# Loading the attention stacks in two halves, the first one slot earlier

## The chip, the cores and the metric

The kernel runs on one core of a Trainium2 chip. The time is the device time of one execution in microseconds; given is the median of three runs. Engines: TensorE (PE, matmuls; PEld is its weight load), VectorE (DVE), ScalarE (ACT), GpSimd (POOL) and SyncE (SP), which here issues all DMA transfers.

## The reference

The input x has 16 batches of 256 tokens with 128 channels. Eight residual blocks follow each other, each on a layer norm of x: a wide attention (16 heads of 64), experts, an attention with heads of eight and a slope bias, experts, a rotary attention with heads of eight, a group attention, a gated recurrence, and the group attention again. The change touches the four attentions with heads of eight. Cut to what matters:

```python
# slope: 16 heads of 8, causal, bias = m * (key - query)
score = einsum('bqhd,bkhd->bhqk', q, k) / sqrt(128) + bias          # causal
# rope: q and k rotated by position, 4 key heads for 16 query heads, causal, output projection
scores = einsum('bqhd,bkhd->bhqk', q, k) * 8 ** -0.5                # causal
# group (twice): a token sees the keys of its own group only; the first 5 tokens see both
l = where(key_mask, einsum('bqhd,bkhd->bhqk', q * scale, k), -inf)
a = softmax(l); out = einsum('bhqk,bkhd->bqhd', a, v)
```

Each of the four is followed by softmax and the product with v.

## The kernel before

The whole program is one launch with a block of instructions per layer, for each engine a list in program order; semaphores order the engines among each other. The four attentions come from one function, `narrow_attention`, with `kind` "slope", "rope" or "group".

**The stack.** A head of eight would fill 8 of TensorE's 128 rows. So q and k in float32 are split into three bf16 parts ("high", "mid", "low"), and for each pair of heads (there are `PAIRS` = 8 pairs, `z` = 0, 1 within a pair, in partitions 0 to 63 and 64 to 127) six combinations of parts are laid below each other: 48 rows that give the product to nearly float32 precision. Below them stand rows for the causal mask, the slope, the group masks (`sp_masks`) and three rows for the row maxima ("shift"). This tile is `st`, with `KEEP` = 3 buffers, index `b % KEEP`; per batch it has two sides (q and k), eight pairs and 256 tokens.

**How it is filled.** POOL writes the parts (`parts`, lines 1014 to 1019). SyncE writes them to a DRAM tensor, `stack_dram`, in rearranged order (pieces "high", "mid", "low", line 613), waits until all six transfers have landed (`parted`) and loads the 48 rows of the stack from there (piece "stack", line 618): one transfer for each `z`, 384 KB each, 4 KB contiguous for each row and side. It also waits until the scores of the batch that used the buffer before are done:

```python
wait(sp, s["scored"], PAIRS * (b - KEEP + 1))
```

In the group layers four transfers of mask rows (line 597) follow behind the stack. The "shift" piece (line 626) writes the row maxima to DRAM, "spread" (line 631) loads them into `st`.

**How it is used.** TensorE computes for each pair i of batch b the "max" piece (line 699: q times k, whose row maxima VectorE takes, line 906) and two batches later the "score" piece (line 720: k times q, with the maxima in the shift rows, which ScalarE puts through exp, line 834), then "value" (line 740). Max 0 of a batch waits for the stack (`landed`) and, in the group layers, for the masks (`masked`); score 0 waits for the spread.

**The order.** `NARROW_ORDER` gives for each kind and engine eight slots; slot i of round n holds score i of batch n and beside it pieces of other batches, as ("piece", index, offset of the batch). The two lines below, of the slope layer, say that SyncE loads the stack of batch n+2 in slot 0 and that TensorE does max 0 of batch n+2 in slot 4 (slot 3 in the rope layer, 4 in the group layers), max 4 in slot 7:

```python
            [("stack", 0, 2)],
            [("score", 4, 0), ("max", 0, 2), ("turnmax", 0, 1), ("turn1", 0, -2), ("max", 1, 2), ("v", 0, 2)],
```

The first `HOSTED` = 2 batches of a layer are prepared while the layer before it runs (`FIRST`).

Of the kernel before, what the change touches and what calls it, by code (L numbers as in the profile page):

```python
# [54 lines left out]
def wait(eng, sem, value):  # L55

    if isinstance(value, int) and value <= 0:
        return
    eng.wait_ge(sem, value)
# [144 lines left out]
def norm_stats(K, s, split=False):  # L204
# [26 lines left out]
    def on_scalar(act):  # L231
# [9 lines left out]
KEEP = 3  # L241
AHEAD = 4
QUADS = H // 4
PAIRS = H // 2
# [50 lines left out]
            [],  # L295
        ],
        "sp": [
            [("stack", 0, 2)],
            [],
            [],  # L300
            [],
            [("shift", 0, 1), ("high", 0, 3)],
            [("mid", 0, 3)],
            [("spread", 0, 1), ("low", 0, 3)],
            [],
        ],
    },
    "rope": {
# [38 lines left out]
            [],  # L347
        ],
        "sp": [
            [("stack", 0, 2)],  # L350
            [],
            [],
            [],
            [("shift", 0, 1), ("high", 0, 3)],
            [("spread", 0, 1)],
            [("mid", 0, 3), ("low", 0, 3)],
            [],
        ],
    },
    "group": {  # L360
# [38 lines left out]
            [("reg_v", 0, 2)],  # L399
        ],  # L400
        "sp": [
            [("stack", 0, 2)],
            [],
            [],
            [],
            [],
            [("shift", 0, 1), ("high", 0, 3)],
            [("spread", 0, 1)],
            [("mid", 0, 3), ("low", 0, 3)],
        ],  # L410
    },
}
# [13 lines left out]
HOSTED = 2  # L426
# [12 lines left out]
FIRST["group"] = FIRST["slope"]  # L439
for _kind in FIRST:  # L440
    FIRST[_kind]["pool"] = [("parts", 0, 0), ("parts", 0, 1)]
    FIRST[_kind]["sp"] = [(_what, 0, _b) for _b in range(HOSTED) for _what in ("high", "mid", "low", "stack")]


EXPERT_HOST = {
# [19 lines left out]
def narrow_attention(nc, K, kind, name, W):  # L465
# [9 lines left out]
    ROW_EXTRA = PARTS * D8  # L475
# [11 lines left out]
    with ExitStack() as ctx:  # L487
        ctx.enter_context(nc.cleanup_on_exit())

        def sb(n, shape, dt=F32):  # L490
# [3 lines left out]
            "stat_dve", "var_ready", "rstd_ready", "norm_ready", "first_dve", "first_var", "first_rstd", "first_norm",  # L494
            "weights", "set_pe", "set_act", "set_pool", "kept0", "kept1", "rows",
            "xn", "full0", "full1", "drained0", "drained1",
            "rotated", "summed", "part", "parted0", "parted1", "landed0", "landed1", "masked0", "masked1", "masked2", "pool_own", "dve_own",
            "maxima", "maxed", "joined", "split", "shifted0", "shifted1", "spread0", "spread1",
            "scored", "exps", "valued", "taken", "biased", "added", "stats",
            "reg_q", "reg_v", "reg_max", "reg_sum", "reg_new", "reg_probs", "reg_out")}  # L500
        full, drained = [s["full0"], s["full1"]], [s["drained0"], s["drained1"]]
        parted, landed = [s["parted0"], s["parted1"]], [s["landed0"], s["landed1"]]
        shifted, spread = [s["shifted0"], s["shifted1"]], [s["spread0"], s["spread1"]]
        masked = [s["masked0"], s["masked1"], s["masked2"]]

# [6 lines left out]
        st = sb("st", [P, KEEP, 2, PAIRS, S], BF16)  # L512
# [51 lines left out]
        LANDED = 16 * 2  # L564
# [35 lines left out]
        def sp_piece(sp, what, i, b):  # L600
            par, turn = b % 2, b // 2
            if what in ("high", "mid", "low"):
                part = ("high", "mid", "low").index(what)
                to = K.stack_dram[par].rearrange("a n d z j s -> a (d z j) n s")
                q_at = (slice(0, 3), slice(3, 6, 2), slice(4, 5))[part]
                k_at = (slice(2, 5), slice(1, 6, 4), slice(0, 1))[part]
                repeat = (3, 2, 1)[part]
                sp.wait_ge(s["part"], 3 * b + part + 1)
                if part == 0:
                    wait(sp, landed[par], LANDED * turn)  # L610
                for which, slots in ((0, q_at), (1, k_at)):
                    src = parts[:, par, part, which, :].unsqueeze(1).to_broadcast([P, repeat, S])
                    sp.dma_start(to[which, :, slots, :], src).then_inc(parted[par], 16)  # L613
            elif what == "stack":
                sp.wait_ge(parted[par], 96 * (turn + 1))
                wait(sp, s["scored"], PAIRS * (b - KEEP + 1))
                for z in range(2):
                    sp.dma_start(st[64 * z:64 * z + ROW_EXTRA, b % KEEP].rearrange("p a j s -> p a (j s)"),
                                 K.stack_dram[par][:, :, :, z].rearrange("a n d j s -> (n d) a (j s)")).then_inc(landed[par], 16)
                if kind == "group" and b >= HOSTED:  # L620
                    sp_masks(sp, b)
            elif what == "shift":
                m, filling = fill["turnmax", b]
                sp.wait_ge(drained[m], filling)
                wait(sp, spread[par], 32 * turn)
                sp.dma_start(K.shift_dram[par].rearrange("r z j s -> (r z j) s"), rows[:, par, :]).then_inc(shifted[par], 16)
            elif what == "spread":
                sp.wait_ge(shifted[par], 16 * (turn + 1))
                for z in range(2):
                    at = slice(64 * z + ROW_SHIFT, 64 * z + ROW_SHIFT + 3)  # L630
                    sp.dma_start(st[at, b % KEEP, 0].rearrange("p j s -> p (j s)"),
                                 K.shift_dram[par][:, z].rearrange("r j s -> r (j s)")).then_inc(spread[par], 16)
# [25 lines left out]
        def pe_piece(pe, what, i, b):  # L658
# [23 lines left out]
            elif what == "max":  # L682
                if i == 0:
                    if b == 0:
                        pe.wait_ge(s["rows"], ROWS_LANDED)
                        pe.wait_ge(s["weights"], 1)
                        wait(pe, s["set_act"], {"slope": 1, "group": 1, "rope": 2}[kind])
                    pe.wait_ge(landed[b % 2], LANDED * (b // 2 + 1))
                    if kind == "group":
                        pe.wait_ge(masked[b % KEEP], 64 * (b // KEEP + 1))  # L690

                wait(pe, s["maxed"], PAIRS * b + i - (1 if b == 0 else 0))
                Mx = max_bank(i, b)
                for t in range(NT):
# [49 lines left out]
            elif what in ("turn0", "turn1"):  # L744
                k = 0 if what == "turn0" else 1
                pe.wait_ge(s["taken"], 2 * b + k + 1)
                for t in range(NT):
                    for g in range(2):
                        ins = pe.transpose(bank[:, (2 * t + g) * P:(2 * t + g + 1) * P],  # L749
                                           ot[:, k, g * S + t * P:g * S + (t + 1) * P], K.ident[:])  # L750
                ins.then_inc(full[m], 1)
            elif what == "turnmax":
                pe.wait_ge(s["split"], b + 1)
                for t in range(NT):
                    ins = pe.transpose(bank[0:48].bitcast(BF16)[:, t * P:(t + 1) * P],
                                       cols[:, b % 2, t].rearrange("p r z j -> p (r z j)"), K.ident16[:])
                ins.then_inc(full[m], 1)
            elif what == "attn":
                for k in ("turn0", "turn1"):
                    pe.wait_ge(drained[fill[k, b][0]], fill[k, b][1])  # L760
                for t in range(NT):
                    ins = pe.transpose(bank[:, t * P:(t + 1) * P], att[:, b % 2, t, :], K.ident[:])
                ins.then_inc(full[m], 1)
            elif what == "project":
                pe.wait_ge(drained[fill["attn", b][0]], fill["attn", b][1])
                for t in range(NT):
                    ins = pe.matmul(bank[:, t * C:(t + 1) * C], att_t[:, b % 2, t * P:(t + 1) * P], W["out"], start=True, stop=True)  # L767
                ins.then_inc(full[m], 1)
            elif what == "reg_scores":
                pe.wait_ge(s["reg_q"], b + 1)  # L770
                pe.wait_ge(landed[b % 2], LANDED * (b // 2 + 1))
                pe.wait_ge(masked[b % KEEP], 64 * (b // KEEP + 1))
                pe.matmul(bank[0:RH, 0:S], qblk[:, b % 2, :], qk[:, b % 2, 1, :], start=True, stop=False)
                pe.matmul(bank[0:RH, 0:S], K.not_first[0:ROW_SHIFT, :], st[0:ROW_SHIFT, b % KEEP, 1, 0, :], start=False,
                          stop=True).then_inc(full[m], 1)
            elif what == "reg_turn":
                pe.wait_ge(s["reg_probs"], b + 1)
                for t in range(NT):
                    ins = pe.transpose(bank[:, t * RH:(t + 1) * RH], pxn[:, t * P:(t + 1) * P], K.ident[0:RH, 0:RH])
                ins.then_inc(full[m], 1)  # L780
            elif what == "reg_value":
                pe.wait_ge(drained[fill["reg_turn", b][0]], fill["reg_turn", b][1])
                pe.wait_ge(s["reg_v"], b + 1)
                for t in range(NT):
                    ins = pe.matmul(bank[:, 0:RH], vplain[:, t, :], pxt[:, t * RH:(t + 1) * RH],
                                    start=(t == 0), stop=(t == NT - 1))
                ins.then_inc(full[m], 1)
# [363 lines left out]
def groups(nc, K, name, W, following):  # L1151
# [3 lines left out]
    with ExitStack() as ctx:  # L1155
# [16 lines left out]
        sim, low, top = sb("sim", [P, TILES]), sb("low", [P, TILES]), sb("top", [P, TILES])  # L1172
# [7 lines left out]
        @block.sync  # L1180
        def _(sp):
            following.sp_first(sp)
            following.first("sp", sp, 8)

        def queries(n):
            return banks[2 + n % 2][:, 0:NT * (C + H)].rearrange("p (t c) -> p t c", t=NT)
# [328 lines left out]
def experts(nc, K, name, W, following):  # L1515
# [3 lines left out]
    with ExitStack() as outer:  # L1519
# [52 lines left out]
        @block.sync  # L1572
        def _(sp):
            following.sp_first(sp)
            following.first("sp", sp, 4 * HOSTED)

        @block.tensor
        def _(pe):
# [756 lines left out]
```

## Time and profile before

| what | value |
|---|---|
| median of three runs | 2356.72 us (2353.28 to 2361.72) |
| span of the profiled execution | 2348.3 us |
| TensorE busy, matmuls | 2052.1 us, 87% |
| TensorE weight loads | 1381.5 us, 59% |
| VectorE, ScalarE, GpSimd busy | 1544.7, 1199.0, 825.0 us |
| granted TensorE clock, mean | 0.932 |
| stack loads | 128 transfers of 384 KB, median 5.5 us to landing |

The profiled execution has no time of its own beside its span; the three runs are timed apart from it. Times in the rows are microseconds from the start of the span. In the span the slope attention runs from about 890 to 1135, the rope attention from 1375 to 1630, the two group attentions from 1680 to 1945 and from 2065 to 2335.

### The profile page before, as it was taken

What the parts mean: (1) busy time and instruction counts of PE and PEld (TensorE: products, weight loads), DVE (VectorE), ACT (ScalarE), POOL (GpSimd) and SP (SyncE); (2) the same over time, 40 slices, a digit from 0 to 9 for tenths busy, and PEclk for the clock granted to TensorE, in tenths of its full rate; (3) what the DMA queues carried; (4) which work ended last, traced back from release to release, by engine and by line L of the source; (5) the groups of instructions that cost most, each with busy time, mean ns of one, the idle gap of its engine ahead of it and who ended that gap; (6) DMA issues with size and microseconds to landing.
All of it is one profiled execution on the core that took longest, in us unless ns stands there. A gap on an engine that the chain in (4) does not pass through costs nothing. (4 is left out here: it accounts for less than half of the span.)

```text
span 2348.3 us, 52692 instructions
## 1 busy us (share of the span) xinstructions
PE 2052.1 (87%) x20735; PEld 1381.5 (59%) x20735; DVE 1544.7 (66%) x2742; ACT 1199.0 (51%) x2044; POOL 825.0 (35%) x1272
## 2 busy tenths in 40 slices
PE   6999999999959997998689989997599985479996
PEld 3666666666648995555578966664345543335553
DVE  5777777777743435666354447774688875768884
ACT  3444444444343324665623326655477776447774
POOL 4444444444423432332144414441233322433330
PEclk9999999999969998999789989998699997769998
DMA  5000000000000022444000214441244420134441
GB/s 167 1 1 1 1 1 1 1 1 1 1 6 2 14 46 70 113 113 99 2 4 1 55 29 113 113 112 32 70 100 115 113 61 1 42 80 107 113 109 46
DMA packets 142787, 120.97 MB, mean 52 GB/s; under 512 B 11808, under 2 KB 127408, under 8 KB 142548
## 3 DMA queue, kind: packets, MB, share of 16 engines
q1 hardware_dynamic: 142548, 117.64, 21.1%
q8 instruction: 167, 2.74, 0.5%
q14 instruction: 72, 0.59, 0.1%
HBM read 63.48 MB, written 54.12 MB: 50 GB/s over the span
## 5 line engine op out<-in xcount | busy, mean ns | idle before, releaser
L906 DVE TENSOR_REDUCE l_group_mx<-maxima 128x4 f32<-128x1024 f32 x248 | 304.0, 1226 | 69.0 <-PE maxima L699 67.5
L834 ACT ACTIVATE l_group_pr<-scores 128x1024 f32<-128x1024 f32 x256 | 261.5, 1021 | 71.7 <-PE scores L720 69.1
L2171 POOL TENSOR_TENSOR l_wide_tiles_sum<-l_wide_pr 128x256 f32<-128x256 f32 x256 | 180.7, 727 | 212.4 <-ACT l_wide_pr L2114 212.4
L2142 DVE RECIPROCAL l_wide_rc<-bank 128x256 f32<-128x256 f32 x128 | 223.8, 1749 | 8.4 <-PE bank L2075 7.9
L2114 ACT ACTIVATE l_wide_pr<-scores 128x512 f32<-128x512 f32 x256 | 139.1, 595 | 163.1 <-PE scores L2058 163.1
L2126 DVE TENSOR_REDUCE l_wide_mx<-maxima 128x2 f32<-128x512 f32 x248 | 159.4, 685 | 52.6 <-PE maxima L2038 52.0
L906 DVE TENSOR_REDUCE l_slope_mx<-maxima 128x6 f32<-128x768 f32 x124 | 118.9, 959 | 74.2 <-PE maxima L706 72.7
L2104 ACT ACTIVATE l_wide_qk<-bank 128x512 f32<-128x512 f32 x128 | 76.4, 597 | 175.2 <-PE bank L2025 175.2
L906 DVE TENSOR_REDUCE l_rope_mx<-maxima 128x6 f32<-128x768 f32 x124 | 118.8, 958 | 56.3 <-PE maxima L706 55.4
L834 ACT ACTIVATE l_slope_pr<-scores 128x768 f32<-128x768 f32 x128 | 103.5, 809 | 87.0 <-PE scores L727 86.8
L834 ACT ACTIVATE l_rope_pr<-scores 128x768 f32<-128x768 f32 x128 | 103.7, 811 | 77.0 <-PE scores L727 76.8
L740 PE MATMUL bank<-l_group_pr,va 128*32 128x256 f32 x2048 | 142.1, 397 | 0.0
L2069 PE MATMUL bank<-l_wide_pr,l_wide_va 128*64 128x256 f32 x1024 | 138.8, 392 | 0.0
L699 PE MATMUL maxima<-l_group_st 50*128 50x256 bf16 x992 | 101.8, 285 | 39.1 <-DVE l_group_mx L906 14.4
L2058 PE MATMUL scores<-l_wide_qk 64*128 64x256 f32 x1024 | 131.4, 376 | 0.0
L2166 POOL CAST l_wide_qk<-l_wide_qk 128x512 bf16<-128x512 f32 x128 | 78.1, 610 | 146.2 <-ACT l_wide_qk L2104 146.2
L1001 POOL CAST l_group_cols<-l_group_mx 128x32 bf16<-128x32 f32 x32 | 6.7, 209 | 318.8 <-DVE l_group_mx L906 318.8
L720 PE MATMUL scores<-l_group_st 53*128 53x256 bf16 x1024 | 102.6, 279 | 16.3 <-ACT l_group_pr L834 11.5
L2058 PEld LDWEIGHTS scores<-l_wide_qk 64*128 64x128 f32 x1024 | 98.6, 189 | 9.8
L1660 ACT ACTIVATE l_rope_e_ht<-maxima 128x512 f32<-128x512 f32 x64 | 38.2, 597 | 106.4 <-PE maxima L1612 106.0
L2025 PE MATMUL bank<-l_wide_xnt,w_q 128*128 128x256 f32 x256 | 90.3, 435 | 2.5 <-ACT l_wide_qk L2104 1.4
L1660 ACT ACTIVATE l_slope_e_ht<-maxima 128x512 f32<-128x512 f32 x64 | 38.2, 597 | 104.4 <-PE maxima L1612 104.1
(468 smaller groups left out, 4853.5 us busy)
## 6 DMA issues: line engine op xcount, KB each, us to landing
l_group_st<-stack_dram SPq DMA_DIRECT2D x64, 384.0 KB, 5.5
l_slope_st<-stack_dram SPq DMA_DIRECT2D x32, 384.0 KB, 5.6
l_rope_st<-stack_dram SPq DMA_DIRECT2D x32, 384.0 KB, 5.5
stack_dram<-l_group_parts SPq DMA_DIRECT2D x64, 192.0 KB, 2.3
stack_dram<-l_group_parts SPq DMA_DIRECT2D x64, 128.0 KB, 1.9
stack_dram<-l_slope_parts SPq DMA_DIRECT2D x32, 192.0 KB, 2.4
stack_dram<-l_rope_parts SPq DMA_DIRECT2D x32, 192.0 KB, 2.3
stack_dram<-l_slope_parts SPq DMA_DIRECT2D x32, 128.0 KB, 2.3
```

What stands on the lines that cost most here:

```text
L699: ins = pe.matmul(Mx[:, z, first:first + keys], st[at, b % KEEP, 0, i, t * P:(t + 1) * P], st[at, b % KEEP, 1, i, 0:keys], start=(t == 0 o ...
L720: ins = pe.matmul(Tp[:, z, t * S:t * S + S - first], st[at, b % KEEP, 1, i, t * P:(t + 1) * P], st[at, b % KEEP, 0, i, first:S], start=(t ...
L740: ins = pe.matmul(Ob[i // 2][32 * z:32 * z + 32, (i % 2) * S + first:(i % 2) * S + S], va[:, b % KEEP, t, h // G, :], pr[:, (h // 2) % AHE ...
L834: act.activation(pr[:, i % AHEAD, :, 0:keys], Tp[:, :, 0:keys], ACT.Exp).then_inc(s["exps"], 1)
L906: dve.tensor_reduce(mx[:, b % 2, :, :, i], max_bank(i, b)[:, :, 0:BLOCKS * keys].rearrange("p z (a k) -> p z a k", k=keys), AX.X, ALU.max, ...
L2025: ins = pe.matmul(bank[:, z * S:(z + 1) * S], w[:, i * P:(i + 1) * P], xnt[:, at, :], start=True, stop=True)
L2058: ins = pe.matmul(Tb[z][:, t * S:(t + 1) * S], qk[rows(z), at, i, 1, t * P:(t + 1) * P], qk[rows(z), at, i, 0, :], start=False, stop=(t == ...
L2069: ins = pe.matmul(Ob[i % 2][rows(z), 0:S], va[:, at, kt, 2 * i + z, :], pr[:, i % 2, z, kt * S:(kt + 1) * S], start=(kt == 0), stop=(kt == ...
L2114: act.activation(pr[:, i % 2, z, :], Tb[z][:], ACT.Exp).then_inc(s["exps"], 1)
L2126: dve.tensor_reduce(mx[:, at, :, 2 * i + z], max_banks(i, b)[z][:].rearrange("p (t k) -> p t k", k=S), AX.X, ALU.max, negate=True).then_in ...
L2142: own.done(dve.reciprocal(rc[:], Ob[i % 2][:, S:2 * S]))
L2171: pool.tensor_tensor(tiles_sum[:, i % 2, z, :], pr[:, i % 2, z, 0:S], pr[:, i % 2, z, S:2 * S], ALU.add).then_inc(s["added"], 1)
```

## The change

Each stack is loaded in two pieces. Piece 0 has pairs 0 to 3, piece 1 pairs 4 to 7; each is two transfers (one for each `z`) of 192 KB, with 2 KB contiguous for each row and side. Piece 1 stays in slot 0 of its round; piece 0 goes one slot ahead, to the end of slot 7 of the round before, where it only needs scores 0 to 3 of the batch that used the buffer. Each piece has a semaphore of its own. TensorE waits for piece 0 at max 0 and for piece 1 at max 4. The masks follow behind piece 1. The register scores of the group layers (`reg_scores`), which read pair 0, wait for piece 0.

```diff
         "sp": [
-            [("stack", 0, 2)],
+            [("stack", 1, 2)],
...
-            [],
+            [("stack", 0, 3)],
...
-            [("mid", 0, 3), ("low", 0, 3)],
+            [("mid", 0, 3), ("low", 0, 3), ("stack", 0, 3)],
...
-    FIRST[_kind]["sp"] = [(_what, 0, _b) for _b in range(HOSTED) for _what in ("high", "mid", "low", "stack")]
+    FIRST[_kind]["sp"] = [(_what, _i, _b) for _b in range(HOSTED) for _what, _i in (
+        ("high", 0), ("mid", 0), ("low", 0), ("stack", 0), ("stack", 1))]
...
                 if part == 0:
-                    wait(sp, landed[par], LANDED * turn)
+                    for half in range(2):
+                        wait(sp, landed[par][half], LANDED * turn)
...
             elif what == "stack":
+                half = slice(i * PAIRS // 2, (i + 1) * PAIRS // 2)
                 sp.wait_ge(parted[par], 96 * (turn + 1))
-                wait(sp, s["scored"], PAIRS * (b - KEEP + 1))
+                wait(sp, s["scored"], PAIRS * (b - KEEP) + half.stop)
                 for z in range(2):
-                    sp.dma_start(st[64 * z:64 * z + ROW_EXTRA, b % KEEP].rearrange("p a j s -> p a (j s)"),
-                                 K.stack_dram[par][:, :, :, z].rearrange("a n d j s -> (n d) a (j s)")).then_inc(landed[par], 16)
-                if kind == "group" and b >= HOSTED:
+                    sp.dma_start(st[64 * z:64 * z + ROW_EXTRA, b % KEEP, :, half].rearrange("p a j s -> p a (j s)"),
+                                 K.stack_dram[par][:, :, :, z, half].rearrange("a n d j s -> (n d) a (j s)")
+                                 ).then_inc(landed[par][i], 16)
+                if kind == "group" and b >= HOSTED and i == 1:
                     sp_masks(sp, b)
...
-                    pe.wait_ge(landed[b % 2], LANDED * (b // 2 + 1))
                     if kind == "group":
                         pe.wait_ge(masked[b % KEEP], 64 * (b // KEEP + 1))
-
+                if i % (PAIRS // 2) == 0:
+                    pe.wait_ge(landed[b % 2][i // (PAIRS // 2)], LANDED * (b // 2 + 1))
```

SyncE in a steady round of the rope layer, before. The waits are named after the first use of a semaphore, so `l1_slope_scored` is the count of scores done and the names that begin with `l0_wide` stand for the parts' semaphores. The stack waits for scores and parts, and then two transfers go out:

```order
L613 DMA stack_dram<-l_rope_parts 128x256 [waits l0_wide_summed]
L613 DMA stack_dram<-l_rope_parts 128x256
L618 DMA l_rope_st<-stack_dram 48x2x2048 [waits l1_slope_scored,l0_wide_biased]
L618 DMA l_rope_st<-stack_dram 48x2x2048
L626 DMA shift_dram<-l_rope_rows 48x256 [waits l1_slope_spread0,l0_wide_scored]
```

The same place with the change:

```order
L616 DMA stack_dram<-l_rope_parts 128x256 [waits l0_wide_summed]
L616 DMA stack_dram<-l_rope_parts 128x256
L622 DMA l_rope_st<-stack_dram 48x2x1024 [waits l1_slope_scored,l0_wide_divided]
L622 DMA l_rope_st<-stack_dram 48x2x1024
L622 DMA l_rope_st<-stack_dram 48x2x1024 [waits l1_slope_scored,l0_wide_divided]
L622 DMA l_rope_st<-stack_dram 48x2x1024
L631 DMA shift_dram<-l_rope_rows 48x256 [waits l1_slope_spread1,l0_wide_scored]
```

Between the same neighbours, the last part and the next shift, two transfers have become four of half the size, and each pair has its own wait for scores.

TensorE at the end of slot 7 of the rope layer, scores 7 and max 4, before:

```order
L720 MATMUL scores<-l_rope_st 128x256 [waits l1_slope_exps]
L720 MATMUL scores<-l_rope_st 128x256
L720 MATMUL scores<-l_rope_st 128x128 x2
L727 MATMUL scores<-corner_kq,choose 128x2x64 x4
L699 MATMUL maxima<-l_rope_st 128x128 [waits l1_slope_maxed]
```

And with the change:

```order
L725 MATMUL scores<-l_rope_st 128x256 [waits l1_slope_exps]
L725 MATMUL scores<-l_rope_st 128x256
L725 MATMUL scores<-l_rope_st 128x128 x2
L732 MATMUL scores<-corner_kq,choose 128x2x64 x4
L704 MATMUL maxima<-l_rope_st 128x128 [waits l1_slope_maxed,l1_slope_landed11]
```

TensorE's matmuls keep their order; max 4 has gained the wait for the second piece.

## Rows read from the trace of the kernel before

**Rows 1.** The page: span, and busy time, share and instructions of each engine
```profile
span 2348.3 us, 52692 instructions
...
PE 2052.1 (87%) x20735; PEld 1381.5 (59%) x20735; DVE 1544.7 (66%) x2742; ACT 1199.0 (51%) x2044; POOL 825.0 (35%) x1272
```

**Rows 2.** Waits of TensorE, whole span: us in total, times, longest us
```profile
PE maxima L699 <- DMA l_group_st<-mask_dram: 12.9, 4, 6.5
...
PE maxima L699 <- DMA l_rope_st<-stack_dram: 10.2, 12, 1.5
...
PE maxima L699 <- DMA l_slope_st<-stack_dram: 9.3, 11, 1.4
...
PE maxima L699 <- DMA l_group_st<-stack_dram: 7.6, 6, 1.9
...
PE maxima L699 <- issue: 3.1, 6, 0.7
```

**Rows 3.** Timeline, SyncE, slope and rope: start, us, line, op, out<-in, count
```profile
1013.53 0.80 SPq L618 DMA_DIRECT2D l_slope_st<-stack_dram  x2
1021.90 0.31 SPq L626 DMA_DIRECT2D shift_dram<-l_slope_rows  x1
...
1027.13 0.81 SPq L618 DMA_DIRECT2D l_slope_st<-stack_dram  x2
...
1084.81 0.81 SPq L618 DMA_DIRECT2D l_slope_st<-stack_dram  x2
...
1560.91 0.81 SPq L618 DMA_DIRECT2D l_rope_st<-stack_dram  x2
```

**Rows 4.** DMA issues, first and second transfer of 1013.53: KB, us to landing
```profile
l_slope_st<-stack_dram SPq DMA_DIRECT2D x1, 384.0 KB, 4.7
...
l_slope_st<-stack_dram SPq DMA_DIRECT2D x1, 384.0 KB, 6.3
```

**Rows 5.** Timeline, TensorE, slope: max 0, max 4, max 0, max 0 [idle before <-releaser]
```profile
1020.23 0.34 PE L699 MATMUL maxima<-l_slope_st 56*128 56x128 bf16 x4 [0.96 <-DMA l_slope_st<-stack_dram]
...
1026.27 0.34 PE L699 MATMUL maxima<-l_slope_st 56*128 56x128 bf16 x4
...
1076.93 0.34 PE L699 MATMUL maxima<-l_slope_st 56*128 56x128 bf16 x4
...
1091.56 0.34 PE L699 MATMUL maxima<-l_slope_st 56*128 56x128 bf16 x4 [0.98 <-DMA l_slope_st<-stack_dram]
```

**Rows 6.** Timeline, TensorE, rope: max 0 of two rounds in a row
```profile
1553.02 0.33 PE L699 MATMUL maxima<-l_rope_st 50*128 50x128 bf16 x4
...
1568.43 0.34 PE L699 MATMUL maxima<-l_rope_st 50*128 50x128 bf16 x4 [1.23 <-DMA l_rope_st<-stack_dram]
```

**Rows 7.** Timeline, SyncE, a group round: the stack and the masks
```profile
1843.51 0.81 SPq L618 DMA_DIRECT2D l_group_st<-stack_dram  x2
1844.36 1.21 SPq L597 DMA_DIRECT2D l_group_st<-mask_dram  x4
```

**Rows 8.** Windows, same round: us, busy (x) by engine, PEclk, DMA share, GB/s
```profile
1850.00:1850.50 0.50, 0.50 (x7) 0.14 (x5) 0.23 (x2) 0.46 (x1) 0.32 (x2) 1.00 0.12 28
```

**Rows 9.** Timeline, TensorE, same round: max 0
```profile
1851.24 0.39 PE L699 MATMUL maxima<-l_group_st 50*128 50x256 bf16 x4 [0.66 <-issue]
```

**Rows 10.** Waits of SyncE, whole span: us in total, times, longest us
```profile
SPq L618 <- DMA stack_dram<-l_group_parts: 46.3, 32, 4.3
...
SPq L59 <- PE scores L727: 12.4, 20, 1.7
```

**Rows 11.** Windows, loads at the start of the program (last two columns: DMA)
```profile
6.00:8.00 2.00, 0.00 (x0) 0.00 (x0) 1.83 (x10) 0.97 (x1) 1.38 (x6) 1.00 1.20 291
...
10.00:12.00 2.00, 0.00 (x0) 0.00 (x0) 1.85 (x10) 0.00 (x0) 1.53 (x6) 1.00 1.02 408
```

**Rows 12.** Windows, a slope round behind a stop of 1.38 us
```profile
976.60:991.33 14.73, 14.10 (x212) 9.23 (x214) 9.77 (x17) 7.71 (x13) 3.48 (x7) 0.88 0.44 111
```

**Rows 13.** Windows, a group round while its stack is loaded
```profile
1800.00:1801.00 1.00, 1.00 (x18) 0.42 (x20) 0.99 (x2) 1.00 (x2) 0.00 (x0) 1.00 1.10 160
```

More of the change, by code:

```diff
@@ L349 @@
         "sp": [
-            [("stack", 0, 2)],
+            [("stack", 1, 2)],
             [],
@@ L356 @@
             [("mid", 0, 3), ("low", 0, 3)],
-            [],
+            [("stack", 0, 3)],
         ],
@@ L401 @@
         "sp": [
-            [("stack", 0, 2)],
+            [("stack", 1, 2)],
             [],
@@ L496, in narrow_attention @@
             "xn", "full0", "full1", "drained0", "drained1",
-            "rotated", "summed", "part", "parted0", "parted1", "landed0", "landed1", "masked0", "masked1", "masked2", "pool_own", "dve_own",
+            "rotated", "summed", "part", "parted0", "parted1", "landed00", "landed01", "landed10", "landed11", "masked0", "masked1", "masked2", "pool_own", "dve_own",
             "maxima", "maxed", "joined", "split", "shifted0", "shifted1", "spread0", "spread1",
@@ L501, in narrow_attention @@
         full, drained = [s["full0"], s["full1"]], [s["drained0"], s["drained1"]]
-        parted, landed = [s["parted0"], s["parted1"]], [s["landed0"], s["landed1"]]
+        parted = [s["parted0"], s["parted1"]]
+        landed = [[s["landed00"], s["landed01"]], [s["landed10"], s["landed11"]]]
         shifted, spread = [s["shifted0"], s["shifted1"]], [s["spread0"], s["spread1"]]
@@ L770, in pe_piece @@
                 pe.wait_ge(s["reg_q"], b + 1)
-                pe.wait_ge(landed[b % 2], LANDED * (b // 2 + 1))
+                pe.wait_ge(landed[b % 2][0], LANDED * (b // 2 + 1))
                 pe.wait_ge(masked[b % KEEP], 64 * (b // KEEP + 1))
@@ L1182, in _ @@
             following.sp_first(sp)
-            following.first("sp", sp, 8)
+            following.first("sp", sp, 5 * HOSTED)
         def queries(n):
@@ L1574, in _ @@
             following.sp_first(sp)
-            following.first("sp", sp, 4 * HOSTED)
+            following.first("sp", sp, 5 * HOSTED)
         @block.tensor
```

## The prediction

> **What bounds the kernel now.** I read the page's totals first: TensorE is busy 87% of a span of 2348.3 us, and no other engine over 66% [rows 1]. So a microsecond in which TensorE stands still counts, unless it is lost again later. Then TensorE's waits by releaser: 9.3 us in the slope layer, 10.2 us in the rope layer and 7.6 us in the two group layers end with the load of a stack, 12.9 us with that of the group masks (its longest one, 6.5 us, and its like are the layers' starts) [rows 2]. All are at line 699, in the first maxima of a batch ("max 0").
>
> Next the timelines, for when a stack is issued (call that T) and when max 0 starts. In the slope round of T = 1013.53 the two transfers are issued 0.4 us apart (0.80 us for two) and land 4.7 and 6.3 us after their own issue, at T+4.7 and T+6.7 [rows 3, 4]. TensorE starts max 0 at 1020.23, T+6.7, after standing 0.96 us [rows 5]: that is the landing of the second transfer. Max 4, the first to read pairs 4 to 7, follows 6.0 us on, at 1026.27 [rows 5].
>
> What fixes T? SyncE works in order: the shift follows max 0, then come the parts, the spread and the stack, which waits until the parts have landed. After max 0 at 1020.23 the shift is issued at 1021.90 and the next stack at 1027.13 [rows 3, 5]. This is a ring: 6.9 us from max 0 to T, 6.7 us to the landing, 13.6 us and more by its jitter. TensorE's own work for a round is as long: from 1076.93, a max 0 without standing, to 1091.56 less its 0.98 are 13.65 us [rows 5]. So each late T shows as standing. In the rope layer the same is 1568.43 - 1553.02 - 1.23 = 14.18 us of own work [rows 6].
>
> The group layers differ. Behind each stack SyncE issues four mask transfers, over 1.21 us [rows 7]. In the round of T = 1843.51 a stack like the one above is down at T+6.8, yet the DMA engines still carry 28 GB/s at a share of 0.12 from 1850.0 to 1850.5, and max 0 starts at 1851.24, T+7.7 [rows 7, 8, 9]. A share of 0.12 is two of sixteen engines: small transfers, the masks, at the end of the queue. The stop has no releaser by name there ("issue", six such, 3.1 us [rows 2]). I read the stack waits of the group layers as mask waits.
>
> **The change, part by part.**
>
> *First half, slope and rope.* It is 384 KB, as much as the one transfer that lands at T+4.7 today; as two pieces 0.4 us apart I put it at T+4.9. When does TensorE want it? In rounds that began without standing: slope, T = 1084.81, max 0 at 1091.56 after 0.98, so TensorE was ready at T+5.8; rope, T = 1560.91, max 0 at 1568.43 after 1.23, ready at T+6.3 [rows 3, 5, 6]. The half is in time by 0.9 and 1.4 us. Its wait for the last scores of the batch in front falls too, which released the stack in 20 rounds, 12.4 us in all [rows 10]. So 9.3 + 10.2 = **19.5 us** of standing go. Do they come back? The two rounds without standing say no: 13.65 and 14.18 us, with nothing in them that took its place. What is late next is the spread before the first scores of the next batch, which stands behind the shift and some parts in SyncE's order and so keeps its distance from max 0.
>
> *Second half.* Issued at T+0.8, or when the scores are done, it completes the same 768 KB and lands about where the stack does now, T+6.7 to T+7.2; max 4 wants it 6 us after max 0. Nothing.
>
> *SyncE.* Two more issues per stack, 2 x 0.4 = 0.8 us. After a stack SyncE has nothing to issue until the next shift, 1014.3 to 1021.9 [rows 3], and that hides them; without this cover a round would pay 0.8. TensorE waits for one semaphore more at max 4, long satisfied: nothing. A layer's first two stacks are loaded well before use: nothing.
>
> *Masks, group layers.* T does not move: all 32 group stacks are released by the landing of their parts [rows 10]. The masks are issued from T+1.7 to T+2.9 instead of T+0.8 to T+2.1, still ahead of T+6.4, when the stack's bytes are through. They gain nothing, since the same bytes lie ahead. They may lose: each engine has 24 runs of 2 KB ahead in place of 12 of 4 KB. The trace has no 2 KB run into this tile, so I bound it by the loads at the program's start. There 512 B runs (x) move at 291 GB/s with a share of 1.20: 16 x 1.20 x 2 us / 1137 runs = 34 ns each; 4 KB runs (the weights) at 408 GB/s with 1.02: 16 x 1.02 x 2 us / 199 = 164 ns each [rows 11]. The part of a run's price that does not go with its bytes is between 0 and 34 ns; the line through both gives (34 - 164/8)/(7/8) = 15 ns, and I take it because 2 KB lies between the two sizes. Twelve more runs per engine: 0 to 0.4 us in each of 26 rounds, 0 to 10.6 us; with 15 ns 0.18 us. About half of the group rounds stand at max 0 at all (6 + 6 + 2 stops [rows 2]), so 14 x 0.18 = 2.5 us, of which a part is taken back by the slack of the others: **1.5 us**.
>
> *Clock.* The slope round from 976.60 to 991.33, behind a stop of 1.38 us, had a granted clock of 0.88 and was 1 us longer than its kind [rows 12]. I count nothing for that and leave 1 us to the range.
>
> Sum: 19.5 - 1.5 = 18.0 us, off the profiled execution's 2348.3 us span. The median of the three times is 2356.72, 8.4 us above that span, and I take this rest as unchanged: 2356.7 - 18.0 = **2338.7 us**.
>
> The rows give 2.0 us for the second 384 KB, and the sum used them. The Trainium skill ("DMA: Bandwidth & Descriptors", section Anatomy of one DMA) fits a transfer as 2.0 us + bytes/436e3, for the GpSimd path; by that, half the bytes save 0.9 us. An estimate by that page has the first half at T+5.9, 0.1 us late in 13 slope rounds, and the sum at 2340. The 4.7 us of the first transfer speak against it: the fit gives 2.9.
>
> **Rivals.**
>
> *The wait table is right for the group layers as well.* Then 27.1 us go [rows 2]: about 2329.6. Against it: max 0 starts at T+7.7 there and at T+6.7 in slope, behind identical stacks.
>
> *Halves served side by side.* If the engines share between queued transfers, the first half lands near T+6.5 and only the late T is won: 3 to 8 us, 2349 to 2354. Against it: of today's two transfers the first is down 2 us before the second. For it: they were issued only 0.4 us apart, and four in flight have not been seen.
>
> *Masks follow their issue.* If their landing goes by their own issue and not by the queue, it slides by up to 0.8 us in 26 rounds: +10 to +21 for 1.5, so 2347 to 2358. Against it: the last mask is issued at T+2.1 and lands five us later.
>
> *A fixed cost per transfer, in line (the other side).* Of the 2.0 us between two landings a part f may be per transfer. Two more transfers put the masks 2f later, 26 x 2f; with f = 0.6 that is +31, so 2356.7 - 19.5 + 31 = 2368. It decides from f = 0.37 us. Against it: while a stack flows the engines' share is 1.10 from 1800 to 1801, with no gap to be seen [rows 13]. The Trainium skill ("DMA: Bandwidth & Descriptors", section Rules for kernel authors) advises transfers of 1 MiB and more because of a fixed cost of each, and if that 2.0 us stood in line the kernel would lose 85 us; its Anatomy section puts most of it in the receipt of the last write, which overlaps.
>
> **How the numbers follow.** Forecast (2335 to 2346) 66%; group layers too 8%; side by side 10%; masks later 10%; fixed cost 6%. What this kernel's measurement can tell from no change is 0.3%, 7 us: below 2349.7. Faster: 0.66 + 0.08 and 0.04 of each of the next two, 0.82. Same: 0.12. Slower, above 2363.8: the fixed cost, 0.06. The range for 8 in 10 leaves out the low end of the second case and the high ends of the last three: 2331 to 2349.
>
> **What would show it.** Stack waits of slope and rope at max 0 gone, first-half transfers landing at T+4.7 to 5.0, rounds of 13.7 and 14.1 us. In the group layers max 0 still at T+7.4 to 7.9 with the same 11 us of standing, now under the masks' name. Wrong if slope and rope rounds keep 14.4 us, if waits for the spread or for POOL's parts grow by what max 0 lost, or if group rounds get longer than 15.5 us.

## The result and the profile after

| | before | the change |
|---|---|---|
| median of four runs | 2355.0 us (2349.44 to 2361.72) | 2316.35 us (2313.75 to 2318.05) |
| ratio, 95% interval | | 0.9834 (0.9815 to 0.9854) |
| span of the profiled execution | 2348.3 us | 2316.3 us |

The kernel became 38.7 us faster, where 18.0 were forecast; 2316.35 lies below the low end of the range, 2331. Of the page after:

```profile
span 2316.3 us, 52936 instructions
...
PE 2046.8 (88%) x20735; PEld 1381.6 (60%) x20735; DVE 1544.5 (67%) x2742; ACT 1199.4 (52%) x2044; POOL 826.4 (36%) x1272
...
q1 hardware_dynamic: 156884, 117.65, 18.8%
```

The engines do the same work as in [rows 1]. The last line is SyncE's DMA queue: packets, MB, share of the 16 engines' span. Before it was

```profile
q1 hardware_dynamic: 142548, 117.64, 21.1%
```

The same bytes, in 10% more packets, now take less packet time (the share adds up the times of all packets, and so can exceed 1 in a window): 0.188 x 2316.3 = 435 us on each of the 16 engines in place of 0.211 x 2348.3 = 495 us. My working has no room for that.

TensorE's waits after, against [rows 2] (us in total, times, longest us):

```profile
PE maxima L704 <- DMA l_group_st<-mask_dram: 13.7, 6, 5.2
...
PE scores L725 <- DMA l_slope_st<-shift_dram: 2.9, 3, 1.2
```

No wait for a stack is left, in any of the four layers. Two of the six mask waits are the layers' starts. The other four are 3.7 us together, this one among them:

```profile
1810.04 0.39 PE L704 MATMUL maxima<-l_group_st 50*128 50x256 bf16 x4 [0.97 <-DMA l_group_st<-mask_dram]
```

Length of 13 rounds of each layer, from max 0 of batch 2 to max 0 of batch 15 (batches count from 0), by TensorE's timeline:

| layer | before, one round | after, one round | gain in 13 |
|---|---|---|---|
| slope | 14.45 us | 13.69 us | 9.9 us |
| rope | 14.73 us | 13.80 us | 12.0 us |
| group, first | 15.32 us | 14.95 us | 4.7 us |
| group, second | 15.46 us | 15.09 us | 4.8 us |

They add up to 31.5 of the 32.0 us between the spans. A group round without any standing takes 14.88 us in both kernels, so what the group layers gained is standing that is gone. Now the stack that [rows 3] to [rows 5] show before, in the slope round of the same place. SyncE after, with T = 1009.31:

```profile
1009.31 1.75 SPq L622 DMA_DIRECT2D l_slope_st<-stack_dram  x4
1016.51 0.31 SPq L631 DMA_DIRECT2D shift_dram<-l_slope_rows  x1
...
1021.75 2.56 SPq L622 DMA_DIRECT2D l_slope_st<-stack_dram  x4
```

Landing of its first and of its last transfer, from their own issue at T and at T+1.3:

```profile
l_slope_st<-stack_dram SPq DMA_DIRECT2D x1, 192.0 KB, 2.8
...
l_slope_st<-stack_dram SPq DMA_DIRECT2D x1, 192.0 KB, 3.8
```

TensorE's max 0 after:

```profile
1014.85 0.33 PE L704 MATMUL maxima<-l_slope_st 56*128 56x128 bf16 x4
```

Two things are to be seen. First, all four transfers go out in one block, although pieces 0 and 1 stand in different slots. It is so in all rounds of all four layers from batch 2 on; in 51 of these 56 the block lasts 1.75 to 1.79 us, with no pause between the pieces, and in the other five, like the one of 1021.75, up to 3.12. From max 0 to the next T it is 1021.75 - 1014.85 = 6.90 us here, as it was before (1027.13 - 1020.23, [rows 3, 5]). That is one of the shortest distances; over the rounds of batches 3 to 15 the mean was 7.64 us before and is 7.87 now in the slope layer, 7.82 and 8.01 in the rope layer. The slot ahead moved no T forward. Second, the whole stack is down at T+1.3+3.8, some T+5.2, where it was T+6.7 [rows 4]: the transfer itself became shorter.

This round is one of the fastest. Over the 26 stacks of batches 3 to 15 of the slope and the rope layer, the last transfer landed at T+6.8 in the median before (T+6.4 to T+7.5) and lands at T+6.0 in the change (T+5.1 to T+6.9). So a stack is down some 0.8 us sooner.

The windows from T, of before in that round and of the change in this one (us, busy (x) by engine, PEclk, DMA share, GB/s):

```profile
1013.53:1016.03 2.50, 2.41 (x45) 1.54 (x42) 1.81 (x2) 2.11 (x4) 0.00 (x0) 1.00 0.55 125
1016.03:1018.03 2.00, 2.00 (x41) 1.34 (x38) 1.87 (x6) 0.98 (x2) 0.11 (x1) 1.00 1.08 207
1018.03:1020.03 2.00, 1.23 (x12) 0.66 (x11) 0.65 (x3) 1.75 (x4) 1.38 (x5) 1.00 0.23 35
```

```profile
1009.31:1011.81 2.50, 2.41 (x46) 1.56 (x44) 1.84 (x3) 2.00 (x4) 0.00 (x0) 1.00 0.45 144
1011.81:1013.81 2.00, 2.00 (x41) 1.32 (x38) 1.87 (x6) 1.01 (x2) 0.14 (x1) 1.00 0.82 221
1013.81:1015.81 2.00, 1.98 (x24) 1.32 (x23) 1.09 (x4) 1.76 (x4) 1.39 (x5) 1.00 0.00 0
```

Before, the packets of the stack take 16 x (2.5 x 0.55 + 2 x 1.08 + 2 x 0.23) = 64 engine-us, and a share of 0.23 is left behind T+4.5; after it is 16 x (2.5 x 0.45 + 2 x 0.82) = 44 and nothing is left. The means of the 26 stacks, over the same 6.5 us from T, are 64 and 49. One or several of three edits could do that: the runs of 2 KB, the number of transfers, or their order. Before, all of partitions 0 to 47 went ahead of all of 64 to 111; now the transfers alternate between the two.

### The profile page after: what moved, and what is told of

Read it like the earlier page. It is cut to its first block and busy times, and to the rows that moved or that the text cites. A ratio compares the mean times of both kernels' runs of the same rounds, so it can differ in the third digit from the quotient of the medians.

```text
span 2316.3 us, 52936 instructions
## 1 busy us (share of the span) xinstructions
PE 2046.8 (88%) x20735; PEld 1381.6 (60%) x20735; DVE 1544.5 (67%) x2742; ACT 1199.4 (52%) x2044; POOL 826.4 (36%) x1272
```

## The experiments

**Each part of the change alone.** Two theories stood against each other: the time comes from the ring (half wait, early issue), or from the way in which the stack is cut. Run e1 has the change with both pieces back in one slot (so for all three kinds); piece 0 still waits for scores 0 to 3 only:

```diff
-            [("stack", 1, 2)],
+            [("stack", 0, 2), ("stack", 1, 2)],
...
-            [("stack", 0, 3)],
+            [],
```

> The change without its earlier issue: both pieces of a stack are issued in slot 0 of the round, piece 0 behind all scores of the batch before only as far as it reads (scores 0 to 3), max 0 waits for piece 0 and max 4 for piece 1. Theory A (the half that max 0 waits for is what counts): T moves by less than 0.6 us, piece 0 lands near T+4.1 and TensorE wants it at T+5.8, so the time stays within 4 us of the change, 2313 to 2320. Theory C (the earlier issue counts): slope and rope rounds go back by the scores' wait, 2325 to 2335.

Measured: 2313.65 us (2312.7 to 2315.86), 0.9831 (0.9804 to 0.9858) of before. The slot ahead brings nothing, as the blocks of four had shown. That e1 lies 2.7 us below the change is no shown cost of it: the two ran on different chips, their times overlap, and against before the ratios are 0.9831 and 0.9834.

Run e2 has the change, but max 0 waits for both pieces:

```diff
-                if i % (PAIRS // 2) == 0:
-                    pe.wait_ge(landed[b % 2][i // (PAIRS // 2)], LANDED * (b // 2 + 1))
+                if i == 0:
+                    for half in range(2):
+                        pe.wait_ge(landed[b % 2][half], LANDED * (b // 2 + 1))
```

> The change, but max 0 waits for both pieces. By the prediction (the same bytes take the same time) the second piece lands at T+6.7 and the stops of slope and rope come back: 2335 to 2345. Theory B (the whole load has become faster, by 1 us a stack): the last piece lands at T+5.6 to T+6, TensorE wants it at T+5.8 to T+6.3, and nearly all of the gain stays: 2316 to 2324.

Measured: 2323.44 us (2319.6 to 2325.03), 0.9868 (0.984 to 0.9896). TensorE's waits at its max 0:

```profile
PE maxima L705 <- issue: 6.1, 11, 1.1
...
PE maxima L705 <- DMA l_rope_st<-stack_dram: 0.7, 1, 0.7
```

These 12 stops, 6.8 us, all in slope and rope, are near what it lost against the change, 7.1 us by the medians and 5.9 by the spans. With the whole stack awaited, 30 to 32 of the 38.7 us remain.

Run e3 has nothing of the change but the cut: the kernel before, one wait, one semaphore, four transfers.

```diff
-        LANDED = 16 * 2
+        LANDED = 16 * 4
...
-                for z in range(2):
-                    sp.dma_start(st[64 * z:64 * z + ROW_EXTRA, b % KEEP].rearrange("p a j s -> p a (j s)"),
...
+                for half in (slice(0, PAIRS // 2), slice(PAIRS // 2, PAIRS)):
+                    for z in range(2):
+                        sp.dma_start(st[64 * z:64 * z + ROW_EXTRA, b % KEEP, :, half].rearrange("p a j s -> p a (j s)"),
```

> The kernel before, with each stack loaded by four transfers of 192 KB with runs of 2 KB instead of two of 384 KB with runs of 4 KB; one semaphore, all four waited for at max 0, issued in slot 0 behind all scores. Theory A: no gain, 2350 to 2360. Theory B: the load is down 1 us earlier, stops in all four layers shrink, 2320 to 2332.

Measured: 2319.02 us (2313.76 to 2325.4), 0.9861 (0.9826 to 0.9896). The queue's row and a stack from T = 1008.55:

```profile
q1 hardware_dynamic: 156884, 117.65, 18.5%
```

```profile
1008.55:1011.05 2.50, 2.41 (x48) 1.51 (x48) 1.91 (x4) 1.79 (x4) 0.00 (x0) 1.00 0.47 155
1011.05:1013.05 2.00, 2.00 (x35) 1.35 (x32) 1.87 (x5) 1.30 (x2) 0.34 (x2) 1.00 0.86 208
1013.05:1015.05 2.00, 1.99 (x25) 1.21 (x23) 1.11 (x3) 1.75 (x5) 1.38 (x5) 1.00 0.00 0
```

By the windows the stack takes 16 x (2.5 x 0.47 + 2 x 0.86) = 46 engine-us. Four transfers alone give 34.6 us against the 2353.66 us that before had on that chip, a little more than the better of the two expectations. What the half wait adds to them is e1 against e3, 5.4 us between the medians; e3's four times lie 12 us apart, its two best (2313.76 and 2314.78) within those of e1, so this is a rough figure. e2 against e1, on the same chip, gives 9.8 us.

**Size of the runs.** Run e4 is e3 cut by side (q, k) and not by pairs, so that the runs stay at 4 KB:

```diff
-                        sp.dma_start(st[64 * z:64 * z + ROW_EXTRA, b % KEEP, :, half].rearrange("p a j s -> p a (j s)"),
+                        sp.dma_start(st[64 * z:64 * z + ROW_EXTRA, b % KEEP, side].rearrange("p j s -> p (j s)"),
```

> As e3 with four transfers of 192 KB, but cut by side, so that each run is 4 KB as before. If the smaller runs are what makes the load faster: the DMA share of a stack as before (65 engine-us) and 2348 to 2358. If it is the number and size of the transfers: as e3, 2320 to 2332.

Measured: 2322.57 us (2320.12 to 2328.77), 0.9873 (0.9841 to 0.9904). Its times overlap those of e3. So the 2 KB runs are not what helps; nor do they show the cost that I gave them.

**The order.** Run e5 is e3 with its two loops exchanged: the same four transfers, those to partitions 0 to 47 first.

```diff
-                for half in (slice(0, PAIRS // 2), slice(PAIRS // 2, PAIRS)):
-                    for z in range(2):
+                for z in range(2):
+                    for half in (slice(0, PAIRS // 2), slice(PAIRS // 2, PAIRS)):
```

> e3 with its four transfers in another order: both halves for partitions 0 to 47 first, then both for 64 to 111, so that transfers to the two sets of partitions no longer alternate. Count, size and runs are those of e3. Theory B1 (the load is faster because transfers to the two sets of partitions are under way at the same time): the flow in the middle of a stack falls back to 170 to 190 GB/s, and the time to 2340 to 2355. Theory B2 (smaller transfers are faster in themselves): as e3, 2314 to 2325.

Measured: 2347.16 us (2336.54 to 2349.54), 0.9958 (0.9935 to 0.9981). The standing came back:

```profile
PE maxima L700 <- DMA l_slope_st<-stack_dram: 9.8, 11, 1.4
...
PE maxima L700 <- DMA l_rope_st<-stack_dram: 8.1, 10, 1.5
...
PE maxima L700 <- DMA l_group_st<-stack_dram: 6.8, 5, 1.8
```

So did the time of the transfer: the queue's row, and a stack from T = 1060.35:

```profile
q1 hardware_dynamic: 156884, 117.65, 20.5%
```

```profile
1060.35:1062.85 2.50, 2.41 (x44) 1.48 (x40) 1.74 (x2) 2.19 (x4) 0.00 (x0) 1.00 0.49 129
1062.85:1064.85 2.00, 2.00 (x41) 1.33 (x40) 1.87 (x6) 0.91 (x2) 0.03 (x1) 1.00 1.07 186
1064.85:1066.85 2.00, 1.31 (x12) 0.74 (x11) 0.72 (x3) 1.76 (x4) 1.38 (x5) 1.00 0.38 54
```

The stack takes 16 x (2.5 x 0.49 + 2 x 1.07 + 2 x 0.38) = 66 engine-us. Count, size, runs, packets and waits are those of e3, and 28 us lie between them. They ran on two chips, but each beside before: e3 gains 34.6 us and e5 6.9, and the intervals of the two ratios lie apart (0.9826 to 0.9896, 0.9935 to 0.9981). The order is what counts.

**More of it.** Run e7 cuts before into eight transfers of 96 KB, alternating:

```diff
-        LANDED = 16 * 2
+        LANDED = 16 * 8
...
+                for quarter in range(4):
+                    some = slice(quarter * PAIRS // 4, (quarter + 1) * PAIRS // 4)
```

> The kernel before with each stack in eight transfers of 96 KB, alternating between the two sets of partitions, 1 KB runs, one semaphore. A fixed cost per transfer in line (the fourth rival) would show as a later landing: issue alone takes 8 x 0.41 = 3.3 us, so the last is issued at T+2.9 and the masks end at T+4.5. If only the issue counts, the last landing comes at T+6 to T+6.5 and the time to 2325 to 2340; if alternation at a finer grain gives more flow, 2318 to 2325; if transfers had a fixed cost in line of 0.4 us or more, 2350 or above.

Measured: 2341.16 us (2331.93 to 2347.67), 0.9944 (0.9924 to 0.9964). That is above what was expected if only the issue counts, and below a fixed cost in line. The packets take least time of all here, and a transfer lands fast:

```profile
q1 hardware_dynamic: 185556, 117.67, 17.2%
...
l_slope_st<-stack_dram SPq DMA_DIRECT2D x128, 96.0 KB, 2.3
```

But eight issues of 0.4 us take SyncE 3.3 us and more: over the 26 stacks the last transfer goes out at T+3.2 in the median and lands at T+6.5, later than the T+5.8 of e3, and the stack waits of slope and rope are back at 6.1 and 7.4 us. Why this costs 22 us against e3, and not those 13.5 alone, the runs don't settle.

**Which side.** In e5 both ends of a transfer are grouped: the SBUF partitions written and the DRAM tensor's rows read. Two runs part them. In both, two quarters of each stack change places, so they compute other products than the kernel's, in the same instructions on the same amounts of data; only their times are of use. Run e9 groups the written side and alternates the read one:

```diff
+                for z, half, from_z, from_half in ((0, 0, 0, 0), (0, 1, 1, 0), (1, 0, 0, 1), (1, 1, 1, 1)):
```

> Four transfers as in e3, all waited for at max 0, but written to partitions 0 to 47 (two), then 64 to 111 (two), while their sources in DRAM alternate between the two heads of the pairs as in e3. Two quarters of each stack thus change places, so other products are computed than the kernel's. If it is the partitions written (SBUF side) that must alternate: as e5, 2338 to 2350. If it is the addresses read (DRAM side): as e3, 2314 to 2325.

Measured: 2338.77 us (2337.34 to 2344.25), 0.9945 (0.9925 to 0.9964), the queue at 20.4%. Run e10 has it the other way round:

```diff
+                for z, half, from_z, from_half in ((0, 0, 0, 0), (1, 0, 0, 1), (0, 1, 1, 0), (1, 1, 1, 1)):
```

> The counterpart of e9: the partitions written alternate as in e3, the sources are grouped as in e5; two quarters of each stack change places here too. SBUF side: as e3, 2314 to 2325. DRAM side: as e5, 2338 to 2350.

Measured: 2324.33 us (2323.28 to 2327.45), 0.9877 (0.9861 to 0.9894), the queue at 18.9%. From e3 (2319.0) to e5 (2347.2) the written side alone costs 20 us; the 5 us of the read side alone lie within the spread of e3. The 26 stacks of batches 3 to 15 of slope and rope show the same two groups:

| run | written | read | last transfer down, median | packet time of a stack, mean |
|---|---|---|---|---|
| before (2 x 384 KB) | grouped | grouped | T+6.8 | 64 engine-us |
| e5 | grouped | grouped | T+6.7 | 60 |
| e9 | grouped | alternating | T+6.6 | 59 |
| e10 | alternating | grouped | T+6.0 | 49 |
| e3 | alternating | alternating | T+5.8 | 47 |

So the most of it lies where the bytes are written.

**The masks.** In e8, built on e1, the masks go out ahead of piece 1, and only 384 KB are in front of them:

```diff
+                if kind == "group" and b >= HOSTED and i == 1:
+                    sp_masks(sp, b)
                 for z in range(2):
...
-                if kind == "group" and b >= HOSTED and i == 1:
-                    sp_masks(sp, b)
```

> e1 with the group masks issued between the two pieces of the stack. If the masks are what max 0 still waits for in the group layers: the steady rounds lose their last stops, 3 to 5 us less than e1, 2308 to 2311. If the group rounds are bound elsewhere: as e1, 2312 to 2316.

Measured: 2312.38 us (2311.23 to 2313.0), 0.9817 (0.9799 to 0.9834). Only the layers' two starts still wait for masks:

```profile
PE maxima L704 <- DMA l_group_st<-mask_dram: 9.9, 2, 5.2
```

The group rounds are 14.88 and 14.87 us, against 14.87 and 15.02 in e1 and 14.95 and 15.09 in the change: they stand no more, but against e1 that is only 2 us, and 1.3 by the medians. The 3 to 5 us that were expected of it did not come; 2312.38 is in the range for "bound elsewhere". Last, the change and this version were timed side by side on one chip.

> The changed kernel once more, beside e12 on the same chip: 2313 to 2319.

> e8 once more, beside the changed kernel: 2311 to 2314, 2 to 6 us below e11 if the later issue of piece 0 and the masks between the pieces are both no loss.

Measured: the change 2316.45 us (2314.66 to 2319.37), 0.9843 (0.9826 to 0.9859); the version with the masks ahead 2310.95 us (2310.04 to 2311.35), 0.982 (0.9804 to 0.9837). It is the fastest of the study, 5.5 us below the change, and their runs don't overlap. It differs from the change in two things, the slot of piece 0 and the masks; how the 5.5 us divide was not measured on one chip.

## Why the prediction was wrong

The direction held; the size was off by 22.4 us: 14.0 us of span (32.0 for 18.0), and the 8.4 us between span and median that I carried over.

**The step that failed** is the one on the second half: it "completes the same 768 KB and lands about where the stack does now, T+6.7 to T+7.2", and on the masks "they gain nothing, since the same bytes lie ahead". I took the time of the stack as a matter of bytes in line. It is also one of which partitions they go to, and in what order. Grouped, 768 KB are down at T+6.6 to T+6.8 in the median (before, e5, e9); alternating, at T+5.8 to T+6.0 (e3, the change). Run e3 has the alternation without the half wait and the early issue, and gives 34.6 us; e5 takes away the alternation alone and is back at 2347 us. In my sum it is above all the term of the masks that failed: the group layers gained 9.5 us where I had a loss of 1.5, which is 11.0 of the 14.0 us; slope and rope gave 2.4 us more than I had.

**First half, slope and rope.** The stops went, as said, and the rounds that began without standing were the right measure for slope: 13.69 us for 13.65. For rope I had 14.18 us as TensorE's own round; it became 13.80, so that single round held more than its stop; what, was not looked into. The first half landed at T+4.2 in the median (T+3.7 to T+5.8), and not at T+4.9. 9.9 + 12.0 = 21.9 us came for 19.5, close, but in part by luck, as most of it has another reason than mine: the whole stack is down at T+6.0 in the median, TensorE wants it at T+5.7 to T+5.9, and so waiting for the half saves 5 to 10 us (e1 against e3 and e2) where I had put all 19.5 down to it.

**The early issue** was credited with the release of 20 waits for scores, 12.4 us. No wait for scores is left among SyncE's, in the change and in e1 alike, but its stack waits for parts grew from 34.8 to 42.8 us in slope and rope: the landing of the parts sets T. The ring that I put at 6.9 us from max 0 to T, by one round, is 7.6 to 7.8 in the mean before and no shorter after. e1 puts the worth of the slot at zero.

**Masks.** The reading was right in kind: the standing of the group layers belonged to the masks, and it kept their name in all four stops that are left. It was wrong in sign and size: -9.5 us where I had +1.5, since the bytes ahead of the masks went through sooner. Before, max 0 behind a stop began at T+7.4 to T+7.9 in a steady group round; in the change the four end at T+5.8 to T+6.9. e3 has group rounds of 14.91 and 15.01 us and e5, grouped, 15.26 and 15.37, so this gain too goes with the order. The dearer 2 KB runs, 0 to 10.6 us, showed nowhere: e3 with 2 KB runs is no slower than e4 with 4 KB.

**SyncE's issues, the clock.** Costed at nothing and rightly so with four transfers; e7 shows where that cover ends. The mean granted clock is 0.932 before and 0.933 after.

**The rest around the span.** I carried 8.4 us over unchanged. The time of the change's profiled execution is 2318.05 us for a span of 2316.3, so only 1.7 us lie around a span. The other 6.7 were the spread of before: its four runs cover 12 us and the profiled execution lay at their fast end. Those of the change cover 4, and there the profiled execution was the slowest, so that the median is just the span, 2316.35. Why runs with fewer stops agree better with each other was not tested.

**The rivals.** That the group layers gain too had 8%; it was nearest in its time (2329.6) and names where a third of the gain was, though not its cause. Side by side: I argued that transfers are served one after the other because two of them landed 2 us apart. That they are not strictly in line is seen in the first 192 KB to partitions 0 to 47: they land at T+3.0 in the median when the next transfer goes to the other set (e3) and at T+3.4 when it goes to the same (e5, e9). So they share, but the alternating order makes the whole faster and not the first half slower. A fixed cost in line: four transfers of the same bytes took less time than two, so f is not 0.37 us; grouped (e5), four are down at T+6.7 in the median, where the two of before are at T+6.8, and f is about nothing. Masks by their own issue: at T+1.7 to T+2.9 they no longer stopped most rounds, so no.

**The two sets of partitions.** What I did not weigh before was this. The loads to 48 partitions run at 186 to 207 GB/s in the middle windows of before and e5, where loads to all 128 partitions ran at 408 [rows 11]. The Trainium skill ("SBUF — State Buffer", section Door 1: The DMA port swizzle) says that partitions 0 to 63 reach only one half of the 16 DMA ports, and 64 to 127 only the other, with 196 GB/s measured for 0 to 63; the trace agrees. Its next rule would have spoken against what was found: the same page ("Can I just issue two DMAs to hit both halves?") and "DMA: Bandwidth & Descriptors" (section Rules for kernel authors) say that two transfers to the two halves serialize and aren't worth it. For two of 384 KB the trace agrees, T+4.7 and T+6.7 [rows 4]; for four of 192 KB in turn the measurement differs, the whole down at T+5.8 to T+6.0 for T+6.8 and 47 to 49 engine-us for 64, and it decides. That the ports are the cause fits e9 and e10 but was not measured by itself.

## What to carry to other kernels

When a tile is loaded in two partition sets like these (0 to 47 and 64 to 111), try to cut each load in two and to issue the parts in turn; here that alone was worth 1.4% (e3). Stop before the issues get long beside the transfer: eight of them, 3.3 us, lost most of it again (e7). Small transfers that something waits for can go ahead of the bulk that is not yet needed (e8, 1 to 2 us here). A move to an earlier slot is worth nothing where another wait sets the issue: look for whether the instructions of both slots start in one block. Judge a landing time by many rounds, not by one, and take a median's distance to a profiled span for what it is, mostly a spread of runs.

## What was unexpected of the hardware

- The time of the same bytes depends on the order of the transfers: four of 192 KB, runs of 2 KB, took the queue 18.5% of the span when alternating between partitions 0 to 47 and 64 to 111, and 20.5% when grouped, with 28 us between the kernels.
- It is mainly the written side: 20.4% with only that side grouped (e9), 18.9% with only the read side grouped (e10).
- Smaller pieces lower the packet time further (96 KB: 17.2%), while the kernel gets slower: each issue takes SyncE 0.4 us, and the last of eight lands at T+6.5 for T+5.8 with four.
